# Writing out the sequence loops of four attention phases, on every engine

## The reference

```
x = x + L0_attn(layernorm(x))                    # causal attention, 16 heads of 16
x = x + L0_xattn(layernorm(x), ctx, mask)        # cross attention, 16 heads of 16
x = x + L0_ffn(layernorm(x))                     # 64 experts, 8 per token, and a shared one
x = x + L1_attn(layernorm(x))                    # causal attention with rotary positions
x = x + L1_xattn(layernorm(x), fside, ctx, mask) # 16 heads of 64, 512 keys
x = x + L1_ffn(layernorm(x))                     # 8 experts, 2 per token
```

## Time and profile before

| what | value |
|---|---|
| median of 3 runs | 4165.12 us (4162.1 to 4169.45) |
| the profiled execution, its own time | 4159.41 us |
| its span, first to last instruction | 4157.3 us |
| L0_attn and L0_xattn (narrow), on PE | 21 to 900 us |
| L1_attn (narrow), on PE | 2045 to 2496 us |
| L1_xattn (wide), on PE | 2501 to 3479 us |

### The profile page before, as it was taken

How to read it: one execution, slowest core, us unless ns; L and a number is a source line. 1 busy time by engine, 2 the same in 40 slices (tenths; PEclk the granted TensorE clock), 3 DMA queues, 4 the chain that set the end, 5 groups by cost and what they waited for, 6 DMA issues and landing times. The chain is left out here.

```text
span 4157.3 us, 94617 instructions
## 1 busy us (share of the span) xinstructions
PE 3697.5 (89%) x31492; PEld 3027.7 (73%) x31492; DVE 2637.5 (63%) x7079; ACT 1849.7 (44%) x3874; POOL 2101.6 (51%) x1962
## 2 busy tenths in 40 slices
PE   6999699976589999899799997999999998699991
PEld 5787577755368888788678875777777776599991
DVE  4777377757964444566466646777777776755543
ACT  2444255532223333323234446766666673255550
POOL 2222212215236666577544425777677773366656
PEclk9999799988799999999899998999999997699995
DMA  1000000000349999899500004233223321465654
GB/s 57 1 0 1 29 11 13 5 19 31 103 161 328 329 328 327 273 322 321 185 2 0 0 1 139 81 93 93 86 84 95 95 73 40 150 220 213 223 182 126
DMA packets 285027, 502.85 MB, mean 121 GB/s; under 512 B 100640, under 2 KB 133536, under 8 KB 274016
## 3 DMA queue, kind: packets, MB, share of 16 engines
q1 hardware_dynamic: 221648, 353.14, 25.3%
q0 software_dynamic: 34464, 94.16, 7.7%
q10 hardware_dynamic: 28656, 52.18, 3.3%
HBM read 367.49 MB, written 131.86 MB: 120 GB/s over the span
## 5 line engine op out<-in xcount | busy, mean ns | idle before, releaser
L592 POOL TENSOR_TENSOR L_xattn_p<-L_xattn_p,L_xattn_rsum 128x1024 f32<-128x1024 f32 x256 | 484.7, 1894 | 270.8 <-DVE L_xattn_rsum L693 270.3
L2075 POOL DMA_INDIRECT L_ffn_xin<-zs,L_ffn_listed x398 | 443.6, 1115 | 245.5 <-issue 113.0
L2473 POOL DMA_INDIRECT L_ffn_back<-ys,L_ffn_slots x320 | 311.7, 974 | 132.9 <-issue 71.0
L1319 ACT ACTIVATE L_attn_pT<-L_attn_bank 128x384 f32<-128x384 f32 x512 | 223.5, 488 | 310.9 <-PE L_attn_bank L1417 172.6
L726 ACT ACTIVATE L_xattn_p<-L_xattn_scores,L_xattn_negmax 128x512 f32<-128x512 f32 x512 | 346.1, 686 | 8.6 <-DVE L_xattn_negmax L632 7.9
L2107 PE MATMUL L_ffn_bank<-L_ffn_xT,L_ffn_w 128*128 128x256 f32 (+1 forms) x1536 | 306.5, 346 | 0.0
L808 PEld LDWEIGHTS L_xattn_turned<-ident,L_xattn_p 128*128 128x128 f32 x2048 | 223.3, 142 | 101.7 <-issue 89.5
L808 PE MATMUL L_xattn_turned<-ident,L_xattn_p 128*128 128x128 f32 x2048 | 284.4, 283 | 6.4 <-POOL L_xattn_p L592 3.2
L2178 ACT ACTIVATE L_ffn_xT<-L_ffn_bank 128x512 f32<-128x512 f32 (+1 forms) x199 | 118.1, 593 | 338.2 <-DVE L_ffn_yo L2378 264.5
L2080 POOL TENSOR_TENSOR L_ffn_w<-L_ffn_w,L_ffn_w 128x2048 fp32r<-128x2048 f32 x39 | 181.2, 4646 | 164.9 <-ACT L_ffn_w L2204 164.8
L796 PE MATMUL L_xattn_scores<-L_xattn_kT,L_xattn_qT 64*128 64x512 f32 x1536 | 249.5, 430 | 15.9 <-ACT L_xattn_p L726 12.2
(11 more groups left out here) (391 smaller groups left out, 10830.5 us busy)
## 6 DMA issues: line engine op xcount, KB each, us to landing
L_ffn_w<-in_L_ffn_w SPq DMA_DIRECT2D x78, 1024.0 KB, 5.5
L_ffn_w<-in_L_ffn_w SPq DMA_DIRECT2D x192, 384.0 KB, 4.9
ys<-L_ffn_yo ACTq DMA_DIRECT2D x199, 256.0 KB, 4.8
kv<-kv_v_row SPq DMA_DIRECT2D x128, 256.0 KB, 4.0
L_xattn_k_raw<-kv SPq DMA_DIRECT2D x128, 256.0 KB, 2.8
L_xattn_v<-kv SPq DMA_DIRECT2D x16, 2048.0 KB, 9.0
kv<-kv_k_row SPq DMA_DIRECT2D x96, 256.0 KB, 4.1
L_xattn_mask<-in_L_xattn_mask SPq DMA_DIRECT2D x256, 64.0 KB, 2.2
```

The lines of the kernel that those rows point to most:

```text
L592: pool.tensor_tensor(p[:, s % 4, :, :], p[:, s % 4, :, :], rsum[:, s % 2, :, None].to_broadcast([P, 2, c.keys]), ALU.mult).then_inc(n_read ...
L1319: act.activation(pT[:, h, 0:WIDTH], t_ps[SLOT[2 * g + i]][:, 0:WIDTH], ACT.Exp, scale=c.scale).then_inc(t_taken, 1)
L2075: pool.indirect_dma_start(xin[j % U][:, t, :], None, zs, bass.IndirectOffsetOnAxis(ap=listed[:, 2 * at + t:2 * at + t + 1], axis=0)).then_ ...
L2473: pool.indirect_dma_start(back[:, i % NG, :], None, ys, bass.IndirectOffsetOnAxis(ap=slots[:, tile, k:k + 1], axis=0)).then_inc(b_in[i % N ...
```

## The change

The three loops are replaced by Python loops, so every engine's instructions stand once for each sequence. The same work is emitted in the same order; the branches go, and all waits and addresses become constants.

```diff
         def over_sequences(eng, body):
-            body(-1, 1)
-            body(0, 0)
-            with eng.Fori(0, B // 2 - 1, 1) as pair:
-                for i in range(2):
-                    body(pair * 2 + 1 + i, (1 + i) % 2)
-            body(B - 1, 1)
-            body(B, 0)
+            for b in range(-1, B + 1):
+                body(b, b % 2)
...
         def over_steps(eng, step):
-            for b in (-2, -1, 0):
-                step(b, b % 2)
-            with eng.Fori(0, (B - 4) // 2, 1) as pair:
-                for i in range(2):
-                    step(pair * 2 + 1 + i, (1 + i) % 2)
-            for b in range(B - 3, B + 1):
+            for b in range(-2, B + 1):
                 step(b, b % 2)
...
-                    load_src(0, 0)
-                    load_src(1, 1)
-                    with sp.Fori(0, B // 2 - 1, 1) as pair:
-                        for u in range(2):
-                            sp.wait_ge(src_split, pair * 2 + u + 1)
-                            load_src(pair * 2 + u + 2, u)
+                    for b in range(B):
+                        if b >= 2:
+                            sp.wait_ge(src_split, b - 1)
+                        load_src(b, b % 2)
```

## The result

| | before | after |
|---|---|---|
| median, five runs each | 4162.1 us | 4141.52 us |
| lowest to highest | 4159.27 to 4169.45 us | 4133.35 to 4149.11 us |
| profiled execution, span | 4157.3 us | 4147.2 us |

The ratio of after to before is 0.9945, with a 95% interval of 0.9927 to 0.9964: faster by 0.4 to 0.7%. The runs' means, 4163.2 and 4140.5 us, are 22.7 us apart, the medians 20.6 us. The profiled execution of after is the slowest of its five runs, so its span understates the gain.

The account below looks back on a forecast made before the run. PE was taken to bound the wide attention, stalling at each loop turn. Gains of 22.0 and 1.2 us sum to 23.2 us, from 4165.12 to 4141.9 us; the 8-in-10 range was 4133 to 4153 us.

Parts of the forecast that it names:

- The wide loop's turns: Wide attention on PE: six taken branches and the lower-clock stretches with them go, gaining 22.0 us, low bound 16 us.
- The narrow loops: Three narrow attentions: fifteen taken branches of 0.2 us and register instructions go, gaining 1.2 us, between nothing and 2.3.
- New loads: Narrow steps 1 to 12: about 100 more instruction packets, q8 growing from 152 to 225 or 230, at no cost.
- the sign that I had set: Narrow attentions: a step longer than 24.8 us would show the forecast wrong.
- DVE's turn: Wide loop: DVE's 2.5 us wait after its branch goes with PE's stall; if it stayed, 13 us of room absorbs it.
- The argument made from it: Wide loop's last turn: PE's branch falls through in 76 ns without a stall, so the taken branch itself is what costs.
- Late loads of code: Narrow phases: instruction loads come late in straight code and stop PE, perhaps 83 us, giving 4226 us; chance 4%.
- no other engine became the pace: Wide phase: rival that other engines, losing their pauses, hold PE; time near 4165 us; 4% together with a cheap-branch case.
- narrow turns cost what wide ones do: Narrow loops: fifteen turns at 3.67 us each would give 55 us more, 4087 us; chance 1%.

Follow-up runs that it names:

- narrow-alone kernel: Only the three narrow attentions and the loads of ctx written out, wide loop kept, against the kernel before: 4164.05 us, ratio 0.9998.

## Why the prediction was right, and where it was not

The mechanism forecast for PE is what the runs show, and the terms are near. That the time, 4141.52 us, meets the forecast's 4141.9 within 0.4 us is luck: the forecast was put on the 4165.12 us of three runs of before, whose median became 4162.1 with five, so 20.6 us by the medians, or 22.7 by the ratio, answer to the 23.2 us forecast, and the runs of either kernel spread over 10 to 16 us. **The wide loop's turns** were set at 22.0 us and gave 23.7 with the small gain of each sequence (57.99 to 57.87 us, 14 x 0.12 = 1.7 us). The range began at 16 us in case something stayed at the six places: nothing did. The statement that no more than 22 us could come out was wrong by this 1.7 us. A PE that is busy throughout can still be quicker: with the other engines written out a PE still in its loop went to 57.68 us per sequence. The split into turns and sequences is that of one execution, since the narrow-alone kernel showed 15.0 us for the same turns.

**The narrow loops** were set at 1.2 us, between nothing and 2.3, and gave 1.6. **New loads** cost next to nothing, as the written-out step 13 had said: q8 brings 208 packets where I expected 225 or 230. One step did trip the sign that I had set, a narrow step longer than 24.8 us, with 24.89, by 0.36 us over its neighbours; whether late code held DVE there is not shown.

**DVE's turn** is the step that failed. I wrote that its 2.5 us wait lies beside PE's stall and goes with it, which holds for the change, where DVE's loop goes too, and that if it stayed, DVE's 13 us of room would take it up, which does not. With PE written out and DVE in its loop the whole gain is gone. DVE's room is a sum over 58 us; its stall holds up a chain of maxima, exponentials, reciprocals and transposes, and PE's own wait at the end of that chain is as long as DVE's stall and 0.2 us more. The forecast came true because the change writes out DVE as well. By my reasoning a change on PE alone would have been given 22 us, and it gained nothing.

**Three readings of rows** were off without moving the sum. One of the six windows with a turn shows PE not busy for 1.87 us, not 2 or more. PE is busy 97 to 100% in the narrow steps, not 94 to 99%. And the last turn, at 3414.8 us, does not stand in a window of 57.99 us but in the stretch after 3409.25. The argument made from it holds all the same: PE's timeline there goes from the value product to the next scores without a gap.

```profile
3414.66 1.95 PE L869 MATMUL L_xattn_bank<-L_xattn_pT,L_xattn_v 128*64 128x256 f32 x16
3416.54 0.73 PE L796 MATMUL L_xattn_scores<-L_xattn_kT,L_xattn_qT 64*128 64x512 f32 x4
```

**The rivals.** Late loads of code showed at most in that one step, and no other engine became the pace. That narrow turns cost what wide ones do is false at the length they had, and true, with more than that price, at twice that length. For PE, therefore, the trace bears out a limit between 1,249 matmuls and weight loads per trip, held, and 1,814, not held. The Trainium skill (Runtime: NRT & Kernel Launch, Instruction fetch mechanics) gives PE room for 2048 instructions in blocks of 256, and other engines for 512. The wide trip, counted in the trace with its register and semaphore instructions, is some 1,940 on PE and 430 on DVE, below both numbers, and is not held; no run here varied the length finely enough to say where the limit lies. The sentence of the Trainium skill, in the same section, that a branch beyond the window held forces a load first agrees with the 0.2 us that became 3.3. The 108 ns of the Trainium skill (Advanced Engine Details and Errata, Control Flow Timing) is near neither price: the trace has 208 ns on PE where the trip is held and 3,670 ns where it is not.

## What to carry to other kernels

Read the branch of each hardware loop by engine, and the instruction queues over its trips: here a loop during which nothing is loaded cost next to nothing, and one whose code is loaded anew paid at every turn. Where two engines stall at the same turn, removing one stall gained nothing or a small part; the gain is there when both are gone, and here two engines' programs written out were enough. An engine's idle share doesn't say that a stall on it is covered: ask how soon its next result is wanted.

## What was not expected of the hardware

DVE's stall at a turn does not stand in its branch, which reads 68 to 74 ns, as it does in PE's, which reads 3.3 to 4.1 us; it shows only as "issue" idle time of 2.2 to 3.0 us ahead of the first instruction of the next trip. And the two engines' stalls cost nearly the same alone as together. Six windows with a turn exceed six without by 22.0 us with both engines in the loop (15.0 in the narrow-alone kernel), by 22.2 and 21.2 us with DVE in it and not PE, and by 18.5 us with PE in it and not DVE; the kernel without either gains the whole.
